# Two routed feed-forward layers merged into one block of programs each, and the first ternary unit split by operand part, in an eight-layer fp32 model kernel

## The chip, the cores and the metric

The kernel runs on one core of one Trainium2 chip. The metric is device time in microseconds (us) of one execution; three executions of the kernel before took 1485.39, 1490.49 and 1509.91 us, so the median is 1490.49 us. Lower is better.

## The reference

The input is a matrix of 1024 tokens by 256 features in fp32. Seven residual layers follow one another, each on the layer-normed stream: attention with 16 heads, a ternary feed-forward layer, a gated delta rule, the ternary layer again, attention, a routed feed-forward layer, latent attention with rotary parts, and the routed layer again. The change touches the two feed-forward kinds, each of which occurs twice.

```python
# ternary feed-forward: D = 256, DE = 1024; each weight is a sign in {-1, 0, 1} times one scale
up = jnp.einsum('bsd,ed->bse', x, wu)
gate = jnp.einsum('bsd,ed->bse', x, wg)
hidden = jax.nn.silu(up) * gate
return jnp.einsum('bse,de->bsd', hidden, wd)

# routed feed-forward: D = 256, hidden H = 704, 8 experts, 2 of them per token, low rank 16
for e in range(NUM_EXPERTS):
    c = jnp.sum(jnp.where(sf == e, wf, 0.0), axis=1)
    lo_up = LORA_ALPHA * (xt @ up_A[e].T @ up_B[e].T)
    lo_gate = LORA_ALPHA * (xt @ gate_A[e].T @ gate_B[e].T)
    h_e = jax.nn.silu(base_up + lo_up) * (base_gate + lo_gate)
    ch = c[:, None] * h_e
    mixed_h = mixed_h + ch
    lora_down = lora_down + LORA_ALPHA * (ch @ down_A[e].T @ down_B[e].T)
out = mixed_h @ w_down.T + lora_down
```

## The kernel before, in words

The residual stream X lies token by token in SBUF (8 tiles of 128 tokens), the normed stream XNT feature by feature (2 tiles of 128 features by 1024 tokens). Every engine runs a program of its own, written out by hand in the order in which its instructions issue; semaphores tie the programs together. A layer consists of one or more *blocks*: a block holds one program per engine, and no engine passes its end before all have reached it. `core.layer_done()` adds a barrier between layers. PSUM has 8 banks of 128 by 512 fp32.

**Ternary layer (`ternary_ffn`, lines 281 to 399, one block, twice).** The weights are signs in bf16. To keep fp32 accuracy the normed input is split into three bf16 parts, high, middle and low (`XP`): ScalarE copies XNT to bf16 (line 337, `x_high`), VectorE subtracts it (line 363, `x_rest`), ScalarE rounds the rest (line 340, `x_mid`), VectorE subtracts again (line 367, `x_low`). This is done for each of two halves of 512 tokens and each of two feature tiles k. Then 16 units (8 tiles of hidden features by two halves) follow: TensorE multiplies up and gate, 6 matmuls of 128x512 each (three parts by two k, line 318), into PSUM bank pair u % 2; ScalarE applies silu (line 346); VectorE forms the hidden value (line 376, `hid`); both split it in three parts for the down product. The first unit of a half waits for `x_low`, and unit u waits for `hid` of unit u - 2. The down product follows, with the norm of the next layer behind it (class `Norm`).

**Routed layer (`routed_ffn`, lines 1988 to 2268, two blocks, twice; the second one, `r1`, ends the kernel).** In the first block TensorE makes router logits, then for 11 pairs (5 hidden tiles for each half of the tokens, and one of 64 features that holds both halves, in partitions 0 to 63 and 64 to 127) the base product of up and gate and, in 22 steps, the low-rank corrections of the first and second expert slot (line 2103). ScalarE applies silu (line 2135), VectorE multiplies weight, gate and silu (lines 2193 and 2198, semaphore `hid`), GpSimd adds the two slots to `mixed_hidden` (line 2115). In the second block TensorE forms the low-rank down sums: 4 matmuls over the 64-row tiles (line 2224), then 20 over the full tiles (line 2229), into banks 0 to 3; VectorE masks and adds them (lines 2259, 2262). Then come 8 output tiles of 7 matmuls each (lines 2237, 2240, 2243) in banks 4 to 7, and the norm or the stores behind them. An fp32 matmul appears as two instructions in the trace. The SP queue loads the first weights of the latent layer at the start of the second block of the first routed layer (`r0`), and in `r1` it stores the result.

Of the kernel before, what the change touches and what calls it, by code (L numbers as in the profile page):

```python
# [10 lines left out]
ALU = mybir.AluOpType  # L11
# [269 lines left out]
def ternary_ffn(nc, core, tag, weights, loads):  # L281
# [7 lines left out]
    x_high, x_rest, x_mid, x_low = (sem("_x_" + n) for n in ("high", "rest", "middle", "low"))  # L289
    h_high, h_rest, h_mid, h_low = (sem("_h_" + n) for n in ("high", "rest", "middle", "low"))  # L290
    proj, act_done, hid, down, added = (sem(n) for n in ("_projected", "_silu", "_hidden", "_down", "_added"))
    with ExitStack() as tmp:
        XP = core.sb("xn_parts", [P, 3, KT, S], BF16, tmp)
        xr = core.sb("xn_rest", [P, KT, S], F32, tmp)
# [7 lines left out]
        with nc.Block() as block:  # L302
# [4 lines left out]
            @block.tensor  # L307
            def _(pe):
                for u, (e, half) in enumerate(units):
                    b = u % 2  # L310
                    if e == 0:
                        pe.wait_ge(x_low, KT * (half + 1))
                    if u >= 2:
                        pe.wait_ge(hid, u - 1)
                    for j, w in enumerate((ups, gates)):
                        for part in range(3):
                            for k in range(KT):
                                last = pe.matmul(psum[:, 2 * b + j, :], w[:, k, e * P:(e + 1) * P],  # L318
                                                 XP[:, part, k, cols(half)],
                                                 start=(part == 0 and k == 0), stop=(part == 2 and k == KT - 1))  # L320
                        last.then_inc(proj, 1)
# [12 lines left out]
            def _(act):  # L334
                for half in range(NH2):
                    for k in range(KT):
# [1651 lines left out]
def routed_ffn(nc, core, tag, w, router_loaded, loaded, all_loaded, next_loads, out_dram=None):  # L1988
# [9 lines left out]
    with ExitStack() as tmp:  # L1998
# [7 lines left out]
        with ExitStack() as tmp2:  # L2006
# [10 lines left out]
            Z = sb2("lora_in", [P, 2, TOPK, S])  # L2017
            sil, gc = sb2("silu", [P, 2, HALF]), sb2("gate_weighted", [P, 2, HALF])
            MD = sb2("mask_differences", [P, S])
            z_in, z_done, up_in, silu, gated, hid, mixed = (sem(n) for n in  # L2020
                ("z_in", "z_done", "up_in", "silu", "gated", "hidden", "mixed"))
            mask_diff = sem("mask_difference")
# [11 lines left out]
            steps = [(0, 0)] + [s for p in range(1, NP) for s in ((p, 0), (p - 1, 1))] + [(NP - 1, 1)]  # L2034
            at = {s: i for i, s in enumerate(steps)}
            with nc.Block() as block:
                @block.tensor
                def _(pe):
                    def lora_in(half):
# [45 lines left out]
                    for p, k in steps:  # L2085
# [15 lines left out]
                        for j, wl in enumerate(("upB", "gtB")):  # L2101
# [2 lines left out]
                                                 start=False, stop=True, skip_group_check=True)  # L2104
                            last.then_inc(up_in, 1)

                @block.gpsimd
                def _(pool):
                    pool.wait_ge(pmax, 1)
# [9 lines left out]
                def _(act):  # L2119
# [11 lines left out]
                    for i, (p, k) in enumerate(steps):  # L2131
                        act.wait_ge(up_in, 2 * i + 1)
                        if i >= 2:
                            act.wait_ge(hid, i - 1)
                        act.activation(sil[:, i % 2, :], psum[:, 2 * (p % BUF), :], ACT.Silu).then_inc(silu, 1)  # L2135

                @block.vector
                def _(dve):
# [61 lines left out]
                        if i == 0:  # L2200
                            lora_masked(1)


        with ExitStack() as tmp2:
            d1 = core.sb("lora_down_second", [P, S], F32, tmp2)
            d_in, d_part, d_done, out_in, added = sem("d_in"), sem("d_part"), sem("d_done"), sem("out_in"), sem("added")
            norm = Norm(core, tag, tmp2) if out_dram is None else None
            with nc.Block() as block:
                @block.sync
                def _(sp):  # L2210
                    if next_loads:
                        next_loads(sp)
                    if out_dram is not None:
                        for p in range(NT // 2):
                            sp.wait_ge(added, 2 * p + 2)
                            sp.dma_start(out_dram[2 * p * P:(2 * p + 2) * P, :].rearrange("(t p) d -> p t d", p=P),
                                         X[:, 2 * p:2 * p + 2, :]).then_inc(core.stored, 16)
                        sp.wait_ge(core.stored, 16 * (NT // 2))

                @block.tensor  # L2220
                def _(pe):
                    for k in range(TOPK):
                        for half in range(NH2):
                            pe.matmul(psum[:, 2 * half + k, :], w["dnA"][LAST[half], NFT - 1, :],  # L2224
                                      H[LAST[half], k, NFT - 1, 0:HALF], start=True, stop=False)
                    for half in range(NH2):
                        for k in range(TOPK):
                            for f in range(NFT - 1):
                                last = pe.matmul(psum[:, 2 * half + k, :], w["dnA"][:, f, :],  # L2229
                                                 H[:, k, f, half * HALF:(half + 1) * HALF],  # L2230
                                                 start=False, stop=(f == NFT - 2))
                            last.then_inc(d_in, 1)
                    for t in range(NT):
                        if t >= 4:
                            pe.wait_ge(added, t - 3)
                        for f in range(NFT - 1):
                            pe.matmul(psum[:, 4 + t % 4, 0:D], MX[:, f, t * P:(t + 1) * P], w["down"][:, f, :],  # L2237
                                      start=(f == 0), stop=False)
                        rows = LAST[t // 4]
                        pe.matmul(psum[:, 4 + t % 4, 0:D], MX[rows, NFT - 1, t % 4 * P:(t % 4 + 1) * P],  # L2240
                                  w["down"][rows, NFT - 1, :], start=False, stop=False)
                        pe.wait_ge(d_done, t // 4 + 1)
                        pe.matmul(psum[:, 4 + t % 4, 0:D], DL[:, t * P:(t + 1) * P], w["dnB"],  # L2243
                                  start=False, stop=True).then_inc(out_in, 1)
                        if norm:
                            norm.pe_behind(pe, t)

                if norm:
                    @block.scalar
                    def _(act):  # L2250
                        norm.act(act)

                @block.vector
                def _(dve):
                    for half in range(NH2):
                        cols = slice(half * HALF, (half + 1) * HALF)
                        for k, o in enumerate((DL, d1)):
                            dve.wait_ge(d_in, 2 * half + k + 1)
                            dve.tensor_tensor(o[:, cols], psum[:, 2 * half + k, :], MASK[:, k, cols],
                                              ALU.mult).then_inc(d_part, 1)  # L2260
                        dve.wait_ge(d_part, 2 * half + 2)
                        dve.tensor_tensor(DL[:, cols], DL[:, cols], d1[:, cols], ALU.add).then_inc(d_done, 1)
                    for t in range(NT):
                        dve.wait_ge(out_in, t + 1)
                        dve.tensor_tensor(X[:, t, :], psum[:, 4 + t % 4, 0:D], X[:, t, :], ALU.add).then_inc(added, 1)  # L2265
# [428 lines left out]
```

## Time and profile before

| quantity | value |
|---|---|
| median of three runs (lowest to highest) | 1490.49 us (1485.39 to 1509.91) |
| the profiled execution's own time | 1484.38 us |
| its span | 1482.7 us |
| TensorE busy | 1353.4 us, 91% of the span |
| VectorE / ScalarE / GpSimd busy | 60% / 47% / 19% |
| mean granted TensorE clock | 0.945 of full |
| lines 2224 to 2243 (chain that ended last) | about 3% of the span together |

The granted clock has two levels, 0.5 (1.2 GHz) and 1.0 (2.4 GHz) of full speed; a value between is a stretch that holds both. A busy TensorE at the lower level does half the work per microsecond. Matmuls overlap at their ends, so the distance from start to start, not the duration, says what one costs in a row of them. All windows are microseconds from the start of the span.

### The profile page before, as it was taken

How to read it: one execution, taken by the hardware profiler on the slowest of the kernel's cores; microseconds unless marked ns; L12 is line 12 of the kernel's file. 1: busy time of each engine (PE TensorE's matmuls, PEld its weight loads, DVE VectorE, ACT ScalarE, POOL GpSimd, SP SyncE). 2: the span in 40 equal slices, each digit the busy share in tenths (PEclk: the TensorE clock that was granted, in tenths of full speed). 3: DMA queues.
4: the chain of work that ended last, by engine and by line, in shares of the span. 5: the costliest groups of instructions: out<-in, count | busy, mean ns of one | idle time of the engine just before them, and what ended most of it. 6: DMA issues, size and time to landing. Idle time of an engine off the chain costs nothing. (4 is left out here: it accounts for less than half of the span.)

```text
span 1482.7 us, 32896 instructions
## 1 busy us (share of the span) xinstructions
PE 1353.4 (91%) x13705; PEld 749.8 (51%) x13705; DVE 891.5 (60%) x2142; ACT 696.5 (47%) x1042; POOL 277.6 (19%) x343
## 2 busy tenths in 40 slices
PE   7999997988679988989999989988699999989989
PEld 3355554464347773644555464445245555564436
DVE  3899994647484456649999555323455555526331
ACT  5577786636463226446777732102344444442110
POOL 4331431001510000043000001101433433200210
PEclk9999998999888989999999989999699999999999
DMA  3223301000300000032221030002100000000000
GB/s 88 66 35 68 68 3 32 2 2 0 114 2 4 16 1 15 1 61 34 37 42 24 3 104 0 0 9 48 20 12 17 15 13 15 7 1 1 1 0 29
DMA packets 33958, 37.48 MB, mean 25 GB/s; under 512 B 9153, under 2 KB 24626, under 8 KB 33810
## 3 DMA queue, kind: packets, MB, share of 16 engines
q1 hardware_dynamic: 33810, 35.39, 10.8%
q8 instruction: 108, 1.77, 0.5%
q14 instruction: 40, 0.33, 0.1%
HBM read 18.43 MB, written 1.07 MB: 13 GB/s over the span
## 5 line engine op out<-in xcount | busy, mean ns | idle before, releaser
L586 DVE TENSOR_REDUCE row_max_pieces<-psum 128x1 f32<-128x512 f32 (+3 forms) x672 | 407.0, 646 | 122.7 <-PE psum L481 120.4
L685 ACT ACTIVATE probs<-psum 128x1024 f32<-128x1024 f32 (+7 forms) x384 | 343.8, 900 | 219.7 <-PE psum L481 219.3
L535 PE MATMUL psum<-probs,v_ones 128*32 128x256 f32 (+1 forms) x2688 | 239.1, 376 | 8.6 <-POOL probs L470 4.2
L481 PE MATMUL psum<-q_all,k_head 97*32 97x512 f32 (+3 forms) x1536 | 193.8, 497 | 3.5 <-issue 3.5
L481 PE MATMUL psum<-k_stack,q_stack 96*32 96x512 bf16 x2048 | 162.7, 387 | 5.3 <-DVE row_max_pieces L586 3.1
L481 PE MATMUL psum<-q_stack,k_stack 97*32 97x512 bf16 x2048 | 160.8, 385 | 0.0
L535 PEld LDWEIGHTS psum<-probs,v_ones 128*32 128x32 f32 x2688 | 88.4, 109 | 85.3 <-POOL probs L470 20.9
L481 PE MATMUL psum<-k_head_bf,q_all_bf 80*32 80x512 bf16 (+3 forms) x768 | 95.3, 342 | 5.6 <-POOL q_all_bf L2511 3.7
L481 PEld LDWEIGHTS psum<-q_all,k_head 97*32 97x32 f32 x1536 | 79.2, 110 | 35.0 <-issue 9.3
L481 PEld LDWEIGHTS psum<-k_stack,q_stack 96*32 96x32 bf16 x2048 | 58.1, 97 | 72.1 <-DVE row_max_pieces L586 20.4
L481 PEld LDWEIGHTS psum<-q_stack,k_stack 97*32 97x32 bf16 x2048 | 59.2, 97 | 50.8 <-ACT probs L685 3.7
L2103 PE MATMUL psum<-lora_in,arena 128*128 128x512 f32 (+1 forms) x192 | 80.0, 595 | 3.4 <-DVE lora_in L2181 3.4
L2135 ACT ACTIVATE silu<-psum 128x512 f32<-128x512 f32 x44 | 26.3, 597 | 118.6 <-PE psum L2103 118.6
L2193 DVE TENSOR_TENSOR gate_weighted<-psum,weight_rows 128x512 f32<-128x512 f32 (+1 forms) x48 | 33.1, 690 | 78.6 <-PE psum L2103 78.5
L2053 PE MATMUL psum<-xn_features,arena 128*128 128x512 f32 (+1 forms) x192 | 79.4, 594 | 0.0
L481 PEld LDWEIGHTS psum<-k_head_bf,q_all_bf 80*32 80x32 bf16 x768 | 37.3, 97 | 52.1 <-issue 24.5
L318 PE MATMUL psum<-xn_parts,w_up_signs 128*128 128x512 bf16 x192 | 49.2, 394 | 10.5 <-DVE xn_parts L367 10.5
L470 POOL TENSOR_SCALAR_AFFINE_SELECT probs<-probs 128x128 f32<-128x128 f32 x128 | 36.9, 293 | 114.5 <-ACT probs L685 114.5
L2115 POOL TENSOR_TENSOR mixed_hidden<-slot_hidden 128x512 f32<-128x512 f32 x22 | 27.8, 1265 | 160.0 <-DVE slot_hidden L2198 160.0
L2103 PEld LDWEIGHTS psum<-lora_in,arena 128*128 128x128 f32 (+1 forms) x192 | 32.2, 181 | 46.8 <-issue 39.8
L2053 PEld LDWEIGHTS psum<-xn_features,arena 128*128 128x128 f32 (+1 forms) x192 | 32.4, 181 | 42.3 <-issue 40.7
L2508 POOL TENSOR_TENSOR q_all<-by_cos_over_by_sin,by_sin_moved 64x512 f32<-64x512 f32 x32 | 40.7, 1270 | 65.2 <-DVE row_max_pieces L586 39.5
(358 smaller groups left out, 2079.7 us busy)
## 6 DMA issues: line engine op xcount, KB each, us to landing
q_stack<-arena SPq DMA_DIRECT2D x32, 96.0 KB, 2.6
k_stack<-arena SPq DMA_DIRECT2D x32, 96.0 KB, 2.6
arena<-gd_g_sums SPq DMA_DIRECT2D x6, 512.0 KB, 6.1
q_stack<-arena SPq DMA_DIRECT2D x32, 64.0 KB, 2.3
k_stack<-arena SPq DMA_DIRECT2D x32, 64.0 KB, 2.3
x_tokens<-in_x SPq DMA_DIRECT2D x4, 256.0 KB, 3.4
k_stack<-arena SPq DMA_DIRECT2D x32, 32.0 KB, 2.3
q_stack<-arena SPq DMA_DIRECT2D x32, 32.0 KB, 2.1
```

The costliest lines, as they stand in the source:

```text
L318: last = pe.matmul(psum[:, 2 * b + j, :], w[:, k, e * P:(e + 1) * P], XP[:, part, k, cols(half)], start=(part == 0 and k == 0), stop=(part ...
L470: pool.affine_select(out=own, in_=own, compare_op=ALU.is_ge, fill=0.0, base=0, pattern=[[1, P]], channel_multiplier=-1).then_inc(masked, 1)
L481: last = pe.matmul(o[j:j + 32], by[:, j:j + 32], rows, **flags)
L535: last = pe.matmul(psum[32 * g:32 * g + VW, PVB, a - g * D:D], V[:, c, h, :], pr[:, n % PB, a:(g + 1) * D], start=(c == 0), stop=(c == (2 ...
L586: last = dve.reduce_max(mx[:, h % 2, qt, i:i + 1], o[:, 0:plain], AX.X)
L685: act.activation(pr[:, n % PB, q_from(c):], psum[:, 2 * (n % 2):2 * (n % 2) + 2, :].rearrange("p a n -> p (a n)")[:, q_from(c):], ACT.Exp, ...
L2053: pe.matmul(psum[rows, 2 * (p % BUF) + j, :], w[wb][:, kk, features], XNT[:, kk, cols], start=(kk == 0), stop=False, skip_group_check=True)
L2103: last = pe.matmul(psum[rows, 2 * (p % BUF) + j, :], w[wl][:, features], Z[:, j, k, cols], start=False, stop=True, skip_group_check=True)
L2115: pool.tensor_tensor(MX[:, f, cols], H[:, 0, f, cols], H[:, 1, f, cols], ALU.add).then_inc(mixed, 1)
L2135: act.activation(sil[:, i % 2, :], psum[:, 2 * (p % BUF), :], ACT.Silu).then_inc(silu, 1)
L2193: last = dve.tensor_tensor(gc[rows, i % 2, :], psum[rows, 2 * (p % BUF) + 1, :], CB[rows, k, cols], ALU.mult)
L2508: pool.tensor_tensor(Q[0:RD, h % QSLOTS, cols(half)], t[0:RD, i % 3, :], moved[:, i % 3, :], ALU.add).then_inc(added, 1)
```

## The change

In the routed layer the two blocks become one: each engine's second program is appended to its first, without the end of block between them. On TensorE the low-rank down sums follow the last up product in another order: the 10 matmuls of half 0, for whose hidden tiles they wait with `hid`; then the 4 of the 64-row tiles; then the 10 of half 1. Their banks are 6 and 7 for half 0, 4 and 5 for half 1 (`D_BANK`), and the output tiles use 6, 7, 4, 5 in turn (`OUT_BANK`), the first four of them after VectorE has read the sums (`d_part`). TensorE waits for GpSimd's `mixed` before the output tiles. The SP queue's loads and stores move into the merged block, so the latent layer's three loads are issued at the start of `r0`. The SBUF of both blocks is now reserved together.

In the ternary layer the copy of feature tile k = 1 to the high part moves from ScalarE to VectorE (semaphore `x_high_last`), and the first unit of a half runs part by part: up and gate of the high part after `x_high`, of the middle part after `x_mid`, of the low part after `x_low`.

```diff
+                    if e == 0:
+                        pe.wait_ge(x_high, half + 1)
+                        pe.wait_ge(x_high_last, half + 1)
+                        for j in range(2):
+                            product(j, 0)
+                        pe.wait_ge(x_mid, KT * (half + 1))
+                        for j in range(2):
+                            product(j, 1)
+                        pe.wait_ge(x_low, KT * (half + 1))
+                        for j in range(2):
+                            product(j, 2)
...
-                    for k in range(KT):
-                        act.activation(XP[:, 0, k, cols(half)], XNT[:, k, cols(half)], ACT.Copy).then_inc(x_high, 1)
+                    act.activation(XP[:, 0, 0, cols(half)], XNT[:, 0, cols(half)], ACT.Copy).then_inc(x_high, 1)
...
+                    dve.tensor_copy(XP[:, 0, 1, cols(half)], XNT[:, 1, cols(half)]).then_inc(x_high_last, 1)
                     for k in range(KT):
-                        dve.wait_ge(x_high, half * KT + k + 1)
+                        dve.wait_ge((x_high, x_high_last)[k], half + 1)
...
+            D_BANK, OUT_BANK = ((6, 7), (4, 5)), (6, 7, 4, 5)
...
+                    def lora_down(half):
+                        for k in range(TOPK):
+                            for f in range(NFT - 1):
+                                last = pe.matmul(psum[:, D_BANK[half][k], :], w["dnA"][:, f, :],
+                                                 H[:, k, f, half * HALF:(half + 1) * HALF],
+                                                 start=(half == 0 and f == 0), stop=(half == 1 and f == NFT - 2),
+                                                 skip_group_check=True)
+                            if half:
+                                last.then_inc(d_in, 1)
+
+                    pe.wait_ge(hid, at[NFT - 2, 1] + 1)
+                    lora_down(0)
+                    pe.wait_ge(hid, len(steps))
+                    for k in range(TOPK):
+                        for half in range(NH2):
+                            last = pe.matmul(psum[:, D_BANK[half][k], :], w["dnA"][LAST[half], NFT - 1, :],
+                                             H[LAST[half], k, NFT - 1, 0:HALF], start=(half == 1), stop=(half == 0),
+                                             skip_group_check=True)
+                            if half == 0:
+                                last.then_inc(d_in, 1)
+                    lora_down(1)
+                    pe.wait_ge(mixed, NP)
...
-        with ExitStack() as tmp2:
...
-            with nc.Block() as block:
```

TensorE at the start of a ternary layer (unit 0, then the next): `w_up_signs` and `w_gate_signs` are the two weights, `xn_parts` the three parts. Before:

```order
L307 UNCONDITIONAL_BRANCH
L318 MATMUL psum<-xn_parts,w_up_signs 128x512 x6
L318 MATMUL psum<-xn_parts,w_gate_signs 128x512 x6
L318 MATMUL psum<-xn_parts,w_up_signs 128x512 x6
L318 MATMUL psum<-xn_parts,w_gate_signs 128x512 x6
```

and now:

```order
L318 MATMUL psum<-xn_parts,w_up_signs 128x512 x2
L318 MATMUL psum<-xn_parts,w_gate_signs 128x512 x2
L318 MATMUL psum<-xn_parts,w_up_signs 128x512 x2
L318 MATMUL psum<-xn_parts,w_gate_signs 128x512 x2
L318 MATMUL psum<-xn_parts,w_up_signs 128x512 x2
L318 MATMUL psum<-xn_parts,w_gate_signs 128x512 x2
L318 MATMUL psum<-xn_parts,w_up_signs 128x512 x6
L318 MATMUL psum<-xn_parts,w_gate_signs 128x512 x6
```

The number of matmuls is the same; up and gate alternate by part in the first unit alone.

VectorE at the same place, now (before, the first and fourth rows are absent, and ScalarE makes both high copies):

```order
L377 CAST xn_parts<-xn_features 128x512
L380 TENSOR_TENSOR xn_rest<-xn_features,xn_parts 128x512 x2
L384 TENSOR_TENSOR xn_parts<-xn_rest,xn_parts 128x512 x2
L377 CAST xn_parts<-xn_features 128x512
L380 TENSOR_TENSOR xn_rest<-xn_features,xn_parts 128x512 x2
L384 TENSOR_TENSOR xn_parts<-xn_rest,xn_parts 128x512 x2
```

TensorE from the last up products of `r1` to the first output tile (`lora_in` enters the last corrections, `slot_hidden` the low-rank down sums). Before:

```order
L2103 MATMUL psum<-lora_in,arena 64x512 x4
L2036 UNCONDITIONAL_BRANCH
L2220 UNCONDITIONAL_BRANCH
L2224 MATMUL psum<-slot_hidden,arena 128x512 x4
L2229 MATMUL psum<-slot_hidden,arena 128x512 x20
L2237 MATMUL psum<-arena,mixed_hidden 128x256 x5
```

and now:

```order
L2135 MATMUL psum<-lora_in,arena 64x512 x4
L2143 MATMUL psum<-slot_hidden,arena 128x512 x10
L2155 MATMUL psum<-slot_hidden,arena 128x512 x4
L2143 MATMUL psum<-slot_hidden,arena 128x512 x10
L2169 MATMUL psum<-arena,mixed_hidden 128x256 x5
```

The branches out of one block and into the next are gone, and the 64-row matmuls (L2224, now L2155) stand between the two halves of the others.

## Rows read from the trace of the kernel before

**Rows 1.** Timeline (start, duration, engine, line, idle before) at the seam of `r0`.

```profile
961.29 5.67 PE L2103 MATMUL psum<-lora_in,arena 128*64 128x512 f32 x20
...
969.20 1.26 POOL L2115 TENSOR_TENSOR mixed_hidden<-slot_hidden 128x512 f32<-128x512 f32 x1 [1.07 <-DVE slot_hidden L2198]
...
970.82 3.50 PE L2224 MATMUL psum<-slot_hidden,arena 64*128 64x512 f32 x8 [3.86 <-PEq L2036]
...
991.52 2.32 PE L2237 MATMUL psum<-arena,mixed_hidden 128*128 128x256 f32 x10
```

**Rows 2.** Line 2103 on TensorE, durations min/median/max, first and last start: window 957:976, whole span.

```profile
L2103 PE MATMUL psum<-lora_in,arena x23: 592/592/697, 956.4 to 966.4; 128*64 128x512 f32 x16, 128*128 128x512 f32 x7
...
L2103 PE MATMUL psum<-lora_in,arena x192: 592/592/697, 894.1 to 1426.9; 128*128 128x512 f32 x160, 128*64 128x512 f32 x32
```

**Rows 3.** Timeline at the seam of `r1`.

```profile
1431.31 3.65 PE L2224 MATMUL psum<-slot_hidden,arena 64*128 64x512 f32 x8 [3.85 <-PEq L2036]
...
1452.17 2.32 PE L2237 MATMUL psum<-arena,mixed_hidden 128*128 128x256 f32 x10
```

**Rows 4.** Stretches: length, busy PE, PEld, DVE, ACT, POOL, granted clock, DMA share, GB/s.

```profile
970.80:973.00 2.20, 2.18 (x6) 1.24 (x8) 0.00 (x0) 1.26 (x1) 0.00 (x0) 0.50 0.43 119
973.00:974.00 1.00, 1.00 (x4) 0.03 (x1) 0.00 (x0) 0.00 (x0) 0.00 (x0) 0.55 0.06 11
...
1431.30:1434.00 2.70, 2.69 (x6) 1.25 (x8) 0.00 (x0) 0.00 (x0) 0.00 (x0) 0.50 0.00 0
1434.00:1435.00 1.00, 1.00 (x5) 0.10 (x1) 0.00 (x0) 0.00 (x0) 0.00 (x0) 0.65 0.00 0
```

**Rows 5.** Timeline in `r0`: cadence of sums and of one output tile.

```profile
978.22 0.19 PEld L2229 LDWEIGHTS psum<-slot_hidden,arena 128*128 128x128 f32 x1 [0.24 <-issue]
978.65 0.19 PEld L2229 LDWEIGHTS psum<-slot_hidden,arena 128*128 128x128 f32 x1 [0.24 <-issue]
...
994.93 2.32 PE L2237 MATMUL psum<-arena,mixed_hidden 128*128 128x256 f32 x10
...
998.35 2.32 PE L2237 MATMUL psum<-arena,mixed_hidden 128*128 128x256 f32 x10
```

**Rows 6.** Timeline at the start of the first ternary layer.

```profile
254.29 1.15 ACT L337 ACTIVATE xn_parts<-xn_features 128x512 bf16<-128x512 f32 x2 [1.13 <-PEq L70]
...
254.95 1.29 DVE L363 TENSOR_TENSOR xn_rest<-xn_features,xn_parts 128x512 f32<-128x512 f32 x2 [3.44 <-ACT xn_parts L337]
255.68 1.23 ACT L340 ACTIVATE xn_parts<-xn_rest 128x512 bf16<-128x512 f32 x2 [0.24 <-DVE xn_rest L363]
...
257.69 2.74 PE L318 MATMUL psum<-xn_parts,w_up_signs 128*128 128x512 bf16 x6 [5.16 <-DVE xn_parts L367]
...
258.27 1.23 ACT L340 ACTIVATE xn_parts<-xn_rest 128x512 bf16<-128x512 f32 x2 [0.32 <-DVE xn_rest L363]
...
260.81 0.69 ACT L346 ACTIVATE silu_up<-psum,ternary_scales 128x512 f32<-128x512 f32 x1
...
261.87 0.75 DVE L376 SCALAR_TENSOR_TENSOR hidden<-psum,ternary_scales,silu_up 128x512 f32<-128x512 f32 x1 [1.65 <-PE psum L318]
...
264.26 1.46 PE L318 MATMUL psum<-xn_parts,w_up_signs 128*128 128x512 bf16 x6
```

**Rows 7.** Timeline at the start of the second ternary layer.

```profile
567.86 2.74 PE L318 MATMUL psum<-xn_parts,w_up_signs 128*128 128x512 bf16 x6 [5.37 <-DVE xn_parts L367]
...
574.65 1.46 PE L318 MATMUL psum<-xn_parts,w_up_signs 128*128 128x512 bf16 x6
```

**Rows 8.** Stretches, columns as in rows 4, around the ternary starts and in the latent layer's setup.

```profile
253.70:255.00 1.30, 0.00 (x0) 0.00 (x0) 0.05 (x1) 0.71 (x2) 0.00 (x0) 0.50 0.06 13
...
1060.00:1080.00 20.00, 15.59 (x94) 5.30 (x97) 6.70 (x26) 5.21 (x7) 7.76 (x9) 0.51 0.04 7
```

**Rows 9.** Timeline: two VectorE copies in SBUF in the latent layer.

```profile
1033.55 0.42 DVE L2440 COPY w_q_rotary<-w_q_rotary 128x512 f32<-128x512 f32 x1
...
1038.91 0.69 DVE L2451 CAST k_features_bf<-k_features 128x1024 bf16<-128x1024 f32 x1 [2.36 <-ACT k_features L2414]
```

More of the change, by code:

```diff
@@ L310, in _, with product @@
                     b = u % 2
-                    if e == 0:
-                        pe.wait_ge(x_low, KT * (half + 1))
                     if u >= 2:
                         pe.wait_ge(hid, u - 1)
-                    for j, w in enumerate((ups, gates)):
-                        for part in range(3):
-                            for k in range(KT):
[L318 to L321, printed above, removed]
+                    def product(j, part):
+                        w = (ups, gates)[j]
+                        for k in range(KT):
+                            last = pe.matmul(psum[:, 2 * b + j, :], w[:, k, e * P:(e + 1) * P],
+                                             XP[:, part, k, cols(half)],
+                                             start=(part == 0 and k == 0), stop=(part == 2 and k == KT - 1))
+                        if part == 2:
+                            last.then_inc(proj, 1)
+                    if e == 0:
[9 more added lines that the diff above has]
+                            product(j, 2)
+                    else:
+                        for j in range(2):
+                            for part in range(3):
+                                product(j, part)
                 for t in range(NT):
@@ L2019, in routed_ffn @@
             MD = sb2("mask_differences", [P, S])
+            d1 = sb2("lora_down_second", [P, S])
+            d_in, d_part, d_done, out_in, added = sem("d_in"), sem("d_part"), sem("d_done"), sem("out_in"), sem("added")
+            norm = Norm(core, tag, tmp2) if out_dram is None else None
+            D_BANK, OUT_BANK = ((6, 7), (4, 5)), (6, 7, 4, 5)
             z_in, z_done, up_in, silu, gated, hid, mixed = (sem(n) for n in
@@ L2036, in routed_ffn, with _ @@
             with nc.Block() as block:
+                @block.sync
+                def _(sp):
+                    if next_loads:
+                        next_loads(sp)
+                    if out_dram is not None:
+                        for p in range(NT // 2):
+                            sp.wait_ge(added, 2 * p + 2)
+                            sp.dma_start(out_dram[2 * p * P:(2 * p + 2) * P, :].rearrange("(t p) d -> p t d", p=P),
+                                         X[:, 2 * p:2 * p + 2, :]).then_inc(core.stored, 16)
+                        sp.wait_ge(core.stored, 16 * (NT // 2))
                 @block.tensor
@@ new lines, in _ @@
+                    lora_down(1)
+                    pe.wait_ge(mixed, NP)
+                    for t in range(NT):
+                        bank = OUT_BANK[t % 4]
+                        if t < 4:
+                            pe.wait_ge(d_part, t + 1)
+                        else:
+                            pe.wait_ge(added, t - 3)
+                        for f in range(NFT - 1):
+                            pe.matmul(psum[:, bank, 0:D], MX[:, f, t * P:(t + 1) * P], w["down"][:, f, :],
+                                      start=(f == 0), stop=False)
+                        rows = LAST[t // 4]
+                        pe.matmul(psum[:, bank, 0:D], MX[rows, NFT - 1, t % 4 * P:(t % 4 + 1) * P],
+                                  w["down"][rows, NFT - 1, :], start=False, stop=False)
+                        pe.wait_ge(d_done, t // 4 + 1)
+                        pe.matmul(psum[:, bank, 0:D], DL[:, t * P:(t + 1) * P], w["dnB"],
+                                  start=False, stop=True).then_inc(out_in, 1)
+                        if norm:
+                            norm.pe_behind(pe, t)
@@ L2201, in _ @@
                             lora_masked(1)
-        with ExitStack() as tmp2:
-            d1 = core.sb("lora_down_second", [P, S], F32, tmp2)
-            d_in, d_part, d_done, out_in, added = sem("d_in"), sem("d_part"), sem("d_done"), sem("out_in"), sem("added")
-            norm = Norm(core, tag, tmp2) if out_dram is None else None
-            with nc.Block() as block:
[L2209 to L2254, printed above, removed]
@@ L2264, in _ @@
                         dve.wait_ge(out_in, t + 1)
[L2265 removed]
+                        dve.tensor_tensor(X[:, t, :], psum[:, OUT_BANK[t % 4], 0:D], X[:, t, :], ALU.add).then_inc(added, 1)
                         if norm:
```

6 lines of the change are left out of this document (4 added, 2 removed).

## The prediction

> **What bounds the kernel now.** I read the totals of the page first: TensorE is busy for 91% of the span and the other engines for 60% at most, so a gain has to come out of TensorE's idle time or out of its stretches at the lower clock. Then the timeline at the four places that the change touches, and the granted clock of the same stretches.
>
> At the seam inside a routed layer [rows 1, 3] the reader sees a hole on TensorE: after the last corrections (line 2103) it sits idle for 3.86 us in `r0` and 3.85 us in `r1`, released by the end of the block. The last thing that the end of the block waits for is GpSimd's sum of the two slots, 969.20 + 1.26 = 970.46, and TensorE starts at 970.82. Nothing in the first 10 low-rank sums needs that sum or even the last up product: they read hidden tiles of half 0. The hole has a second price [rows 4]: the granted clock is 0.50 when TensorE resumes, in `r0` until about 973.9 (0.55 over 973 to 974 means slow for 0.9 of it) and in `r1` until about 1434.7 (0.65 over 1434 to 1435, slow for 0.7).
>
> At the start of a ternary layer [rows 6, 7] TensorE waits 5.16 and 5.37 us for the low part of its input, while the high part has been there since about 254.95. It then starts at the lower clock: [rows 8] show 0.50 from 253.7 on, and six matmuls take 2.74 us, where at the higher clock six take 1.46 us.
>
> **The merged routed block.** Costs from start to start: full-height fp32 matmul instructions follow each other by 978.65 - 978.22 = 0.43 us [rows 5]. The output tile shows what a change between full-height and half-height tiles costs: tiles follow by 998.35 - 994.93 = 3.42 us, their 14 instructions of 256 columns are half of 0.43 each, 3.0 us, and two changes remain, 0.2 us each.
>
> In `r0` the last correction starts at 966.4 [rows 2]; 0.43 for itself and 0.2 for the change of tile shape give 967.0 as the first low-rank sum's start, against 970.82: 3.8 us. Its wait for `hid` is for a step some ten steps old. The lower clock goes as well, since TensorE does not stop: 973.9 - 970.82 = 3.1 us at half rate, of which half, 1.55 us, comes back. Against that stands one change of tile shape more, because the 64-row matmuls now have full-height ones on both sides: -0.2 us. Net 5.15 us. In `r1` the last correction starts at 1426.9 [rows 2], so the first sum would start at 1427.5 instead of 1431.31 [rows 3], 3.8 us; the clock gives (1434.7 - 1431.31) / 2 = 1.7 us; the change of shape -0.2. Net 5.3 us. Both layers 10.45 us. That the whole stretch up to the first output tile then shrinks from 20.7 us [rows 1] to about 19.3 us (40 instructions by 0.43, the eight half-height ones in pairs as four by 0.43, two changes) is the same account.
>
> Could a new wait take this back? The wait for the whole `hid` stands behind 20 instructions, 8.6 us: it is reached at 975.6, and GpSimd's sum, which needs the last `hid`, was over at 970.46 [rows 1]. The wait for `mixed` comes another 10 us later. VectorE gets half 0's sums while TensorE multiplies half 1's, so `d_part` and `d_done` are early: half 0's are due about 976.5 to 978.5 and the first output tile starts near 986.3. Bank 4 and 5 are read by VectorE within about 2 us of 986.3, and the third output tile, the first to use one, comes 6.8 us after the first. ScalarE has nothing between its last silu and the norm, so a table load there is covered. The SP queue's three loads move from 970 to about 868 in `r0`; their reader starts at 1024, and their tiles are free in both cases. I cost them at nothing; with the routed weights still in flight they would delay only the router's start. Ending a block later or earlier costs the other engines nothing, since TensorE is last in the merged one too.
>
> **The ternary starts.** Now: ScalarE copies k = 0 (254.29 to 254.9) and VectorE k = 1 at the same time. VectorE's copy is not in this trace; the nearest rows [rows 9] are an fp32 copy of 128x512 in 0.42 us and a cast of twice the size in 0.69 us, so it lies between 0.35 and 0.69; I take 0.42, the row of the same size. Either way TensorE can start at about 254.97, 2.7 us sooner. Its four high matmuls at half rate (0.427) end at 256.7. The middle part is ready at 255.68 + 1.23 = 256.91 [rows 6], a stop of 0.3 us; the low part is ready at 257.63 as before, when TensorE is still at the middle. So far the unit gains 2.4 us or more.
>
> But what ends the gain is unit 2, which needs the hidden value of unit 0, and that needs silu, which ScalarE can only begin after its share of half 1's split. That chain becomes longer: VectorE's copy for half 1 stands ahead of its subtraction, and ScalarE's rounding follows the subtraction directly [rows 6] (the second row of line 340, idle until VectorE). Silu 0, with its table load ahead, moves from 260.81 to 260.81 + 0.36 (a copy of 0.42, less the overlap of queued VectorE instructions) = 261.17; it takes 0.69, and VectorE's product, 0.75, ends at 262.65. TensorE starts unit 2 at about 262.7 instead of 264.26: 1.55 us, the most that the first layer can give. In the second, unit 2 started 574.65 - 567.86 = 6.79 us after unit 0 [rows 7], against 6.57 in the first, so the most is 1.75 us.
>
> Whether TensorE itself is ready at 262.7 is the clock's affair. In the four cases at hand (both ternary starts and [rows 4]) the clock came back 2.9 to 3.4 us after TensorE resumed. If it moves with the earlier start, to about 258.1, units 0 and 1 are over by 261.9 and the caps of 1.55 and 1.75 hold: 3.3 us. If it stays where it was, at 260.6 (8 slow matmuls and the fast ones after them), units 0 and 1 end at 257.0 + 3.6, with 12.4 matmuls done and 11.6 to go at 0.215, so at 263.1: 1.2 us in each layer, 2.4 in all. I take the middle, 2.9 us. The Trainium skill ("TensorE: Matmul & The Clock Gate", Part 1: The HAM clock gate) says that the point of return depends on where the first matmul lands and not on the number of matmuls, which speaks for the second value: by it the sum is 0.5 us smaller. The trace does not decide, since the return came at 2.9 us in one case and 3.4 in another.
>
> From unit 2 on nothing changes: TensorE needs 2.59 us for a unit (264.26 for the first start of unit 2, and six matmuls in 1.29), and the others need less.
>
> **The sum.** 1484.38 - 10.45 - 2.9 = 1471.0 us for an execution like the profiled one. That one is 1.0 us under the fastest of the three timed runs and 6.1 under their median; I add 1.0 for the offset and forecast 1472 us. With the ternary caps it is 1471.6, with the clock staying 1472.5, and with VectorE's copy at 0.69 some 0.5 us more.
>
> **Rivals.** (a) *The half-height matmuls do not run in pairs at the higher clock, or the tile changes cost more.* At the lower clock eight of them take 3.50 us [rows 1], 0.43 each, which can only be pairs of 0.86; at the higher one I count pairs of 0.43. Against: pairs in the corrections' last tile already run so (20 instructions in 5.67 us). If they stay at 0.43 each, 1.7 us per layer is lost: 1475 us. Chance 0.10. (b) *The merged programs do not do what they say*: TensorE is held at the seam by a stop that the trace of before hides under the block's end, for one the last `hid` if the sums of half 0 were not ready. Twice 3.8 us are lost then, 1472 + 7.6 = 1480 us, and with the clock down again 3 us more. The hidden values of half 0 were made tens of microseconds before, so 0.05. (c) *Clock for the better elsewhere.* In the latent layer's setup TensorE runs at 0.51 of the clock for 20 us while busy for 15.6 of them [rows 8]; everything there comes 8 us earlier now. If such a stretch returns to the higher clock early, up to 15.6 / 2, about 8 us, is gained: 1464 us. Nothing says which way it goes, so 0.10. (d) *Slower.* The same mechanism turned round: the gated delta rule and the latent setup both have gaps on TensorE, and if the shift leaves it at the lower clock for longer there, each microsecond of busy TensorE costs half of one. It decides from 2 x 13.3 = 27 us of added low clock on; with 40 us the time is 1485.4 + 20 - 13.3 = 1492 us. The longest such stretch of before is about 20 us, so 0.04. The forecast itself has the remaining 0.71.
>
> **Numbers.** 1472 us. The range 1463 to 1483 holds the forecast with its bounds (1469 to 1475), (a), (b) and (c), and the few microseconds by which a median of timed runs stands above the profiled execution; outside are (d) and runs above 1483. A change of 2%, about what a measurement of this kernel can tell from none, would be 30 us; the forecast is 1.2% under the median of before. For over 2% faster, (c) would have to come at both places: 0.04. Over 2% slower needs more than (d): 0.02. Within 2%: 0.94.
>
> **What would show it.** Right: TensorE without idle time between the last corrections and the first low-rank sum, granted clock 1.00 there, and about 19.3 us from that sum to the first output tile, in both routed layers; TensorE's first ternary matmul at 2.7 us less after the layer's start, a stop of about 0.3 us before the middle part, and unit 2 behind VectorE's product with TensorE idle for less than 1 us before it. Wrong: idle time at the seam with `hid` as its releaser; the 64-row group at 0.43 us each; silu 0 later than 0.7 us against before; or a difference in the attention or delta stages, with another clock, larger than 3 us.

## The result

The changed kernel took 1475.03 us (median of four runs, 1469.18 to 1498.48; three of them lie between 1469.18 and 1478.69); its ratio to the kernel before is 0.990 (95% interval 0.9873 to 0.9926). Run again over five rounds it gave 0.9909 (0.9877 to 0.9941). So it is 0.9 to 1.0% faster, and both intervals lie wholly under 1. The profiled execution took 1471.36 us (span 1469.6), against 1484.38 (1482.7). Some executions of these kernels are about 20 us longer, in the traces of `e4`, `e6`, `e8` and `e9` by a delta stage of 256 to 259 us at a mean granted clock of 0.79 against 234 to 238 us at 0.87 to 0.89; the ratios leave them out, and why they were seven of twelve in `e8` (median of all 1487.91 us) is open.

Each layer ends with the norm of the next one. Cut at the end of each norm into stages, the traces give this, length in us and mean granted clock (the last two columns are the runs `e1` and `e2`, described below):

| stage | before | change | change again | routed part only | ternary part only |
|---|---|---|---|---|---|
| attention A | 238.87 (0.98) | 237.63 (0.99) | 237.63 (0.99) | 239.39 (0.98) | 237.89 (0.99) |
| **ternary, first** | 73.64 (0.94) | 72.13 (0.95) | 72.04 (0.95) | 73.65 (0.94) | 72.09 (0.95) |
| delta rule | 236.32 (0.87) | 234.13 (0.89) | 237.48 (0.87) | 236.13 (0.88) | 237.87 (0.87) |
| **ternary, second** | 73.86 (0.95) | 72.06 (0.97) | 72.05 (0.97) | 73.91 (0.94) | 72.52 (0.95) |
| attention C | 229.91 (0.97) | 228.54 (0.98) | 228.49 (0.98) | 230.13 (0.97) | 231.94 (0.96) |
| **routed r0** | 156.88 (0.95) | 151.61 (0.97) | 151.61 (0.97) | 151.65 (0.96) | 158.02 (0.94) |
| latent | 303.72 (0.94) | 309.53 (0.92) | 304.32 (0.93) | 304.27 (0.93) | 309.11 (0.92) |
| **routed r1** | 155.20 (0.96) | 149.68 (0.97) | 150.64 (0.95) | 150.61 (0.95) | 154.97 (0.95) |

The four touched stages lose 1.5, 1.8, 5.3 and 5.5 us, 14.1 in all; the others, whose programs did not change, differ by -1.2, -2.2, -1.4 and +5.8, at another mean granted clock each.

The seam of `r0` in the timeline of the change (start, duration, engine, line, idle before), answering to [rows 1, 2]:

```profile
953.15 5.67 PE L2135 MATMUL psum<-lora_in,arena 128*64 128x512 f32 x20
...
958.75 8.85 PE L2143 MATMUL psum<-slot_hidden,arena 128*128 128x512 f32 x20
...
961.06 1.26 POOL L2188 TENSOR_TENSOR mixed_hidden<-slot_hidden 128x512 f32<-128x512 f32 x1 [1.07 <-DVE slot_hidden L2273]
967.53 1.99 PE L2155 MATMUL psum<-slot_hidden,arena 64*128 64x512 f32 x8
...
969.45 8.85 PE L2143 MATMUL psum<-slot_hidden,arena 128*128 128x512 f32 x20
...
978.14 2.32 PE L2169 MATMUL psum<-arena,mixed_hidden 128*128 128x256 f32 x10
```

No TensorE row has idle time in its bracket. GpSimd's last sum, which the end of the block used to wait for, now starts 2.3 us into 8.8 us of low-rank sums and ends 3.6 us into them. The eight half-height matmuls take 1.99 us, not 3.50. From the last corrections' first matmul to the first output tile it is 978.14 - 953.15 = 24.99 us; before, 991.52 - 961.29 = 30.23. In `r1` it is the same, with the row of before first and two of the change behind it:

```profile
1421.79 5.67 PE L2103 MATMUL psum<-lora_in,arena 128*64 128x512 f32 x20
...
1414.16 5.67 PE L2135 MATMUL psum<-lora_in,arena 128*64 128x512 f32 x20
...
1439.14 2.32 PE L2169 MATMUL psum<-arena,mixed_hidden 128*128 128x256 f32 x10
```

That is 1439.14 - 1414.16 = 24.98 us, and 1452.17 - 1421.79 = 30.38 before, with the output tile of [rows 3]. The trace of the change again (`e5`) has 24.99 us at both seams. The granted clock (stretch, length, busy PE, PEld, DVE, ACT, POOL, clock, DMA share, GB/s) at both seams, against 0.50 in [rows 4]:

```profile
958.80:967.50 8.70, 8.70 (x22) 3.68 (x20) 2.07 (x3) 1.11 (x1) 2.46 (x2) 1.00 0.00 0
...
1419.80:1439.10 19.30, 19.30 (x50) 8.29 (x49) 4.84 (x7) 0.00 (x0) 2.47 (x2) 1.00 0.00 1
```

The start of the first ternary layer, answering to [rows 6]:

```profile
253.05 0.63 ACT L353 ACTIVATE xn_parts<-xn_features 128x512 bf16<-128x512 f32 x1 [1.13 <-PEq L70]
253.07 0.43 DVE L377 CAST xn_parts<-xn_features 128x512 bf16<-128x512 f32 x1 [2.80 <-PEq L70]
...
253.73 1.03 PE L318 MATMUL psum<-xn_parts,w_up_signs 128*128 128x512 bf16 x2 [2.44 <-ACT xn_parts L353]
...
259.11 1.58 PE L318 MATMUL psum<-xn_parts,w_up_signs 128*128 128x512 bf16 x6
...
259.90 1.51 ACT L362 ACTIVATE silu_up<-psum,ternary_scales 128x512 f32<-128x512 f32 x2
...
261.82 1.46 PE L318 MATMUL psum<-xn_parts,w_up_signs 128*128 128x512 bf16 x6
```

and of the second, answering to [rows 7]:

```profile
559.53 0.63 ACT L353 ACTIVATE xn_parts<-xn_features 128x512 bf16<-128x512 f32 x1 [1.35 <-PEq L70]
...
563.52 0.59 PE L318 MATMUL psum<-xn_parts,w_up_signs 128*128 128x512 bf16 x2
...
566.39 1.26 ACT L362 ACTIVATE silu_up<-psum,ternary_scales 128x512 f32<-128x512 f32 x2
...
568.00 1.47 PE L318 MATMUL psum<-xn_parts,w_up_signs 128*128 128x512 bf16 x6 [0.87 <-DVE hidden L393]
```

The last row of each is unit 2. In the trace of before the first bf16 copy of the second layer is this row (that of the first is in [rows 6]):

```profile
564.46 1.15 ACT L337 ACTIVATE xn_parts<-xn_features 128x512 bf16<-128x512 f32 x2 [1.34 <-PEq L70]
```

Counted from the first bf16 copy unit 2 starts at 8.77 us (9.97 before) and at 8.47 (10.19 before): gains of 1.20 and 1.72. The silu of unit 0 (silu 0) starts at 6.85 and 6.86 us. The granted clock of three stretches, columns as above, says when the clock came back:

```profile
253.70:257.40 3.70, 3.56 (x8) 1.02 (x9) 3.60 (x7) 1.79 (x4) 0.00 (x0) 0.50 0.82 235
...
259.10:260.40 1.30, 1.30 (x7) 0.63 (x6) 0.21 (x1) 1.29 (x2) 0.00 (x0) 0.90 0.00 0
...
562.20:563.50 1.30, 1.30 (x4) 0.53 (x5) 1.30 (x4) 0.46 (x1) 0.00 (x0) 0.64 0.16 55
```

A mean of 0.90 over 1.3 us is 0.26 us at the lower level, so the clock came back at 259.4 in the first layer; 0.64 is 0.94 us, so at 563.1 in the second. In the first layer the whole of unit 0 ran at the lower clock (5.4 us from 253.73 to 259.11) and TensorE has no idle time before unit 2: the clock was the limit. In the second the clock was back in the middle of unit 0, and TensorE idles 0.87 us for the hidden value: the silu chain was the limit.

### The profile page after: what moved, and what is told of

The parts are those of the page before. It is cut to its first block and busy times, and to the rows that moved or that the text cites. A ratio compares the mean times of both kernels' runs of the same rounds, so it can differ in the third digit from the quotient of the medians.

```text
span 1469.6 us, 32878 instructions
## 1 busy us (share of the span) xinstructions
PE 1352.2 (92%) x13705; PEld 746.5 (51%) x13705; DVE 893.1 (61%) x2146; ACT 694.1 (47%) x1038; POOL 277.0 (19%) x343
```

## The experiments

**Routed part alone** (`e1`): the changed kernel with the ternary function of before.

> The changed kernel with the ternary layer of before: only the merged routed block is left. My account of the seam (3.8 us of idle time, 1.6 us of clock, less 0.2 us, per layer) expects 10.5 us under the kernel before, ratio 0.993, and each routed layer 5.2 to 5.5 us shorter in its trace. The rival that the gain of the whole comes from a luckier clock in layers nobody touched expects the routed layers to shorten all the same, but the total to differ from 10.5 us by whatever delta and latent do (they moved by -2.2 and +5.8 us in the changed kernel).

Measured: ratio 0.9932 (0.9912 to 0.9951), about 10 us; `r0` 5.2 and `r1` 4.6 us shorter, every other stage within 0.6 us of before (table). The stage of `r1` gained less than the 5.2 to 5.5 us expected, here as in the change again, at a mean granted clock of 0.95 where the first trace of the change has 0.97; its seam was the same. The account of the seam holds without any help from the layers nobody touched.

**Ternary part alone** (`e2`): the kernel before with the changed ternary function.

> The kernel before with the ternary layer of the change. My account expects 2.9 us less in all (2.4 to 3.3), ratio 0.998, which is at the limit of what five rounds tell from none; in the trace unit 2 of each layer starts 1.2 to 1.75 us earlier after the first bf16 copy. If the gain in the first ternary layer is set by the clock and in the second by silu, as the trace of the changed kernel reads, TensorE idles before unit 2 only where its clock came back within some 3.5 us of its start.

Measured: 0.9994 (0.9974 to 1.0014), not told from no change. Its ternary stages are 1.55 and 1.34 us shorter, as expected; but latent came out 5.4 and attention C 2.0 us longer in its trace. The lower clock lasted until unit 1 in both layers, and no idle time stands before unit 2, which starts 8.75 and 8.95 us after the first copy: the limit was the clock twice. The run tests the ternary part as a whole; what the copy on VectorE and the order part by part give each by itself was not run.

**What the idle time at the seam costs in clock** (`e3`): the kernel before, and behind the last corrections

```diff
+                    for _ in range(4):
+                        pe.matmul(psum[:, 2 * BUF, :], ident[:], XNT[:, 0, 0:HALF], start=True, stop=True)
```

> The kernel before with four fp32 matmuls of 128x512 added on TensorE behind the last corrections, ahead of the end of the first routed block: identity by the normed stream, into bank 6, never read. They fill the 3.8 us of idle time with work that serves nothing. If the lower clock after the seam is the price of the idle time, the granted clock stays 1.00, the eight half-height matmuls take about 1.9 us instead of 3.5 and the kernel gains 1.5 us per layer, 3 us in all, less 0.1 to 0.3 us per layer if the added work ends after GpSimd's sum. If the clock falls for another reason (the end of a block as such), there is no gain and perhaps 0.5 us of loss.

The timeline on TensorE, and the clock of the half-height matmuls:

```profile
967.85 3.70 PE L2107 MATMUL psum<-xn_features,identity 128*128 128x512 f32 x8
971.85 1.99 PE L2226 MATMUL psum<-slot_hidden,arena 64*128 64x512 f32 x8 [0.30 <-PEq L2036]
```

```profile
971.80:973.80 2.00, 1.95 (x9) 0.81 (x9) 0.00 (x0) 1.28 (x1) 0.00 (x0) 1.00 0.42 108
```

The end of the block is still there and the clock stays up, so the end of a block does not lower it by itself; with TensorE idle for 3.86 us there it fell, with 0.30 us it did not. The half-height group takes 1.99 us instead of 3.50. From the corrections' first row to the first output tile both layers gain, 1.4 us in `r0` and 1.6 in `r1`; the stages are 1.46 and 0.78 us shorter. The times do not bear this out: the ratio is 0.9997 (0.9985 to 1.0009), and the 3 us expected, 0.998, lie just outside. In the trace latent took 307.2 us, 3.5 more than before, so what the clock is worth at the seam rests on the seams of the traces alone.

**Merge without the new order** (`e4`): the changed kernel with the half-height sums first, behind `hid` of the last step.

> The changed kernel, but the low-rank sums in the order of before: the four over the 64-row tiles first, behind the wait for the last hidden value, then the twenty others. It splits the gain of the merge from that of the new order. TensorE waits from about 966.8 to 969.2 in the time of the trace of before, 2.4 us per layer; one change of tile shape less gives 0.2 us back. If the clock stays up over 2.4 us: 2.2 us per layer more than the changed kernel, 4.4 us in all. If the clock falls there too: 3.8 us per layer, 7.6 us in all, and almost nothing is left of the merge but its 1.5 us of idle time per layer.

```profile
985.63 1.99 PE L2142 MATMUL psum<-slot_hidden,arena 64*128 64x512 f32 x8 [2.22 <-DVE slot_hidden L2264]
```

TensorE waits 2.22 us for the last hidden value and the clock stays up (1.99 us again). From the corrections' first row to the first output tile it takes 27.07 us in both layers, 2.1 us more than with the change; the stages are 153.71 and 151.82 us. Of the 5.3 us in `r0` the merge alone gives 3.2 and the order 2.1. Ratio 0.9941 (0.9916 to 0.9966), as expected above that of the change, though its interval and those of the change overlap.

**The change again** (`e5`), unaltered:

> The changed kernel itself, unaltered, for a narrower interval and a second trace. My account expects 13.4 us less than before, ratio 0.991, and the four touched stages 1.5, 1.8 or 1.3, 5.3 and 5.5 us shorter as in its first trace. The latent stage took 303.7 us in the trace of before and 309.5 in that of the change. If that is a cost of the change (its loads issued 100 us earlier, or the place where the layer now starts), it is again 309 to 310 us; if it is the clock's chance, it lies anywhere between 303 and 311.

Its latent stage took 304.32 us, against 309.53 in the first trace; the three rows of the latent stage, before, change and change again, differ in granted clock and busy TensorE, not in the number of its instructions:

```profile
1023.78:1327.50 303.72, 279.54 (x3168) 146.10 (x3168) 158.59 (x580) 127.50 (x213) 103.39 (x200) 0.94 0.09 18
```

```profile
1010.39:1319.92 309.53, 286.13 (x3168) 148.52 (x3168) 158.64 (x580) 127.39 (x214) 103.02 (x200) 0.92 0.09 18
```

```profile
1013.74:1318.06 304.32, 282.26 (x3168) 147.02 (x3168) 158.65 (x580) 127.50 (x214) 103.21 (x200) 0.93 0.10 18
```

The same program has it either way, so the difference is no price of the change. One stretch at the lower clock makes it up (first trace of the change, then the change again):

```profile
1042.00:1074.00 32.00, 27.59 (x157) 10.91 (x161) 11.88 (x45) 7.65 (x10) 11.01 (x15) 0.50 0.03 5
...
1045.00:1068.00 23.00, 18.59 (x85) 7.12 (x89) 8.80 (x34) 4.90 (x7) 10.13 (x12) 0.50 0.03 7
```

With its ends it lasts 34.1 us (1041.0 to 1075.1) in the one and 23.9 us (1044.4 to 1068.3) in the other. These are 10.2 us more at the lower clock, with TensorE busy for most of them, and the stage is 5.2 us longer. What ended the stretch later in the one is open.

**The latent layer's loads where they were** (`e6`): `sp.wait_ge(mixed, NP)` ahead of `next_loads(sp)`.

> The changed kernel, but the SP queue waits for GpSimd's last sum of the slots before it issues the latent layer's three loads, which puts them where they stood before. If their early issue costs anything (in the router's start or in the latent stage), this one is faster than the changed kernel by it, 5.8 us if the whole of the latent stage's difference hangs on it. I expect no difference, within 1.5 us of the changed kernel.

Measured 0.9905 (0.9882 to 0.9928), the change's own ratio; `r0` 151.29 us, latent 305.59. Their earlier issue costs nothing that can be seen.

**Three more copies in the silu chain** (`e10`, one execution), ahead of the second half's copy:

```diff
+                    if half:
+                        for e in (NE - 3, NE - 2, NE - 1):
+                            dve.tensor_copy(HP[:, 2, e, cols(half)], XNT[:, 1, cols(half)])
```

> The changed kernel with three more VectorE copies of 128x512 to bf16 (into a tile that is written over later) ahead of the one that begins the second half's split, so the suspected step of the silu chain is four times its size. If unit 2 waits for silu 0 and that for VectorE's copies, silu 0 starts 3 x 0.35 = 1.05 us later, 7.9 us after the first bf16 copy instead of 6.85, and unit 2 starts 9.4 to 9.5 us after it in both ternary layers, instead of 8.77 and 8.47, whatever the clock does. If the clock alone sets the start of unit 2, it stays between 8.4 and 8.8.

The first bf16 copy of the first layer starts at 254.40, of the second at 564.26; unit 2 in each:

```profile
263.89 1.47 PE L318 MATMUL psum<-xn_parts,w_up_signs 128*128 128x512 bf16 x6 [0.58 <-DVE hidden L396]
...
573.73 1.47 PE L318 MATMUL psum<-xn_parts,w_up_signs 128*128 128x512 bf16 x6 [0.20 <-DVE hidden L396]
```

9.49 and 9.47 us after the copy, with silu 0 at 7.87 and 7.86: both as expected, although the clock came back 6.2 us after the copy in one layer and 7.0 in the other. Unit 2 starts at the later of two things, TensorE's own readiness and the chain through VectorE's copy and silu 0.

**The second half's split later** (`e7`): its eight operations go, one by one, behind units 1 to 5 (on VectorE `later = {1: lambda: high(1), 2: lambda: rest(1, 0), ...}`).

> The changed kernel, but in the ternary layer the split of the second half of the tokens is spread over the first units on ScalarE and VectorE instead of standing ahead of them. Silu of unit 0 then follows its table load at about 3.9 us after the first bf16 copy instead of 6.85. If that chain is what TensorE idles for before unit 2 (0.87 us in the second ternary layer's trace, nothing in the first, where the clock was late), this gains 0.9 us there and nothing in the first: 1 us in all, not to be told from the changed kernel by the times, but the idle time before unit 2 must be gone. If VectorE or ScalarE has no room for the eight operations among the units, TensorE waits for hidden values in units 3 to 8 instead and the layer is longer by up to 5 us.

The second ternary layer, unit 1's gate and unit 2:

```profile
565.97 1.46 PE L318 MATMUL psum<-xn_parts,w_gate_signs 128*128 128x512 bf16 x6
567.27 1.46 PE L318 MATMUL psum<-xn_parts,w_up_signs 128*128 128x512 bf16 x6
```

The idle time is gone, unit 2 starts 7.45 us after the first copy instead of 8.47, and that stage takes 71.44 us instead of 72.06; the first stage is unmoved (72.11). As expected the times don't show it: 0.9913 (0.9899 to 0.9927).

**TensorE kept busy in the norms' gaps** (`e8`), on top of `e7`, behind each of the last two groups of transposes:

```diff
+                for _ in range((5, 5)[p - self.PAIRS + 2]):
+                    pe.matmul(self.core.psum[:, spare, 0:P], self.core.ident[:], self.core.ones_sq[:], start=True, stop=True)
```

> The kernel with the later split, and besides 5 small fp32 matmuls (identity by a matrix of ones, 128x128, never read) behind each of the last two groups of transposes in every norm that follows a product. They occupy TensorE in gaps of 1.5 us where it has nothing to do. If the lower clock at the start of the ternary and routed layers comes from these gaps, it stays up: the ternary layer's first two units take 5.2 us instead of up to 8.1 (2 to 2.5 us per layer), and the router's 32 narrow matmuls take 3.5 us instead of 7, so up to 10 us over the kernel, less 0.3 us per norm (seven norms) by which the last group delays the end of the block. If the barrier between the layers is what lets the clock fall, nothing is gained and 2 us are lost.

Measured 0.9887 (0.985 to 0.9924), an interval that overlaps that of `e7`. The router's 32 narrow matmuls take 4.50 us in `r0` instead of 6.81 in the change, but the clock falls while they run, and the first products behind them (6.25 us, 5.53 in the change) are slower. Still `r0` takes 150.49 us and `r1` 146.98, against 151.61 and 149.68 to 150.64 in the two traces of the change. In the first ternary layer the clock fell in unit 0, 2.1 us after a start at the higher level, and nothing was gained there (72.51 us). In the second it stayed up throughout, and the stage takes 71.05 us.

**And in the gaps of the ternary start** (`e9`), three small matmuls ahead of unit 0 and three before its middle part:

> The kernel with the later split and the filled norm gaps, and besides three small fp32 matmuls (never read) on TensorE ahead of the first unit of the ternary layer and three more between its high and its middle part, which fill the 0.9 and 0.95 us that the trace of the kernel with filled norm gaps shows there. If the clock then stays at 1.00 through units 0 and 1, each ternary layer's first two units end 1 to 1.7 us earlier and the whole is 2 to 3 us under that kernel. If it falls all the same, the six small matmuls cost up to 1.4 us per layer and the ternary stages are longer.

```profile
256.53 0.59 PE L324 MATMUL psum<-xn_parts,w_up_signs 128*128 128x512 bf16 x2
...
262.77 1.46 PE L324 MATMUL psum<-xn_parts,w_up_signs 128*128 128x512 bf16 x6
```

```profile
255.80:262.80 7.00, 6.78 (x37) 3.86 (x38) 3.75 (x6) 4.92 (x8) 0.00 (x0) 1.00 0.52 172
```

These rows are of the first ternary layer. The clock stays at 2.4 GHz through units 0 and 1, and the ternary stages take 70.83 and 71.05 us (72.51 and 71.05 in `e8`, 72.13 and 72.06 in the change). So the six added matmuls gained 1.7 us in the first layer and nothing in the second, where the clock had stayed up without them; the expectation had a gain in each. `r1` takes 150.24 us, so its gain in `e8` was not repeated. Ratio 0.9846 (0.9809 to 0.9882), median 1465.14 us: the lowest here. Its interval meets that of the repeated change only in the last 0.05%, but overlaps that of `e8` widely, so the times do not tell `e9` from `e8`.

## Why the prediction was right and wrong

*The seam.* Forecast: first sum 5.7 us after the corrections' first row (966.4 + 0.63 - 961.29), 19.3 us from there to the first output tile, 5.15 and 5.3 us gained. Measured: the first sum at 5.60 us, then 978.14 - 958.75 = 19.39; gained 30.23 - 24.99 = 5.24 in `r0` and 30.38 - 24.98 = 5.40 in `r1`. The whole stage of `r1` gained 5.5 us in the first trace and 4.6 in the other two, at a lower mean clock there. Two parts show by themselves: the clock's 1.5 us in the traces of `e3`, though not in its times, and in `e4` the wait for the last hidden value (2.2 us of the 3.8 of the whole stop; the rest is GpSimd's sum and the end of the block). Half-height matmuls do run in pairs at the higher clock, so rival (a) fell, and with no stop at the seam so did (b).

*The ternary starts.* Forecast 2.9 us between 2.4 and 3.3; measured at unit 2, 1.20 + 1.72 = 2.92; the two stages are 3.3 us shorter, and the 0.4 us between the two are not accounted for. That 2.9 came out is partly luck: I took the middle of two cases, and the first layer hit the clock's bound (1.2) and the second the silu chain's (1.75). In `e2` both layers hit the clock's, 1.22 and 1.24. The chain's own figures held: VectorE's cast takes 0.43 us (forecast 0.42), silu 0 came at 6.85 us (forecast 6.88), and `e10` moved it as computed. I let the clock return at 258.1 or 260.6, that is 3.1 or 5.6 us after TensorE resumed, the same in both layers. It returned after 5.6 us in the first (259.4 - 253.7) and 2.9 in the second (563.1 - 560.2), so each value was right in one layer. The trace of before had shown no case longer than 3.4, and the four cases of it could not tell the two apart.

*What else moved.* The loads, which I costed at nothing, cost nothing that `e6` shows. The untouched stages moved by +1.0 us in sum, but alone by -2.2 to +5.8. Rivals (c) and (d) named the mechanism, a luckier or unluckier clock in delta and latent, and (d) took the longest stretch at the lower clock to be about 20 us; it is 23.9 us in the trace of before (1055.8 to 1079.7) and 34.1 in the first of the change. The two traces of the change differ by 3.4 us in delta and 5.2 in latent, so this is scatter between executions of one program, and no run shows it as an effect of the change.

*The step that failed* is the last one, the reading of size: "A change of 2%, about what a measurement of this kernel can tell from none". The sum was 13.35 us against an execution of 1484.38, 0.90%, and 0.90 to 1.00% was measured. But I set 1472 against the median of before, which stood 6 us above the profiled execution, called that 1.2%, and by the 2% treated it as a change that would not be told from none, with 0.94 for a result within 2%. The 2% had no row behind it. The measured intervals reach 0.1 to 0.4% either way (the change itself 0.27 and 0.32%), so a change of 1% can be told, and was: 0.990 (0.9873 to 0.9926), faster. With a sum resting on idle time that the trace shows four times, "faster by about 0.9%" was the forecast to make. The predicted time itself, 1472, was 3 us under the median of the four runs, inside its range, and next to the profiled execution's 1471.36. The mechanism and the terms of the sum held.

## What to carry to other kernels

The seam between these two blocks cost its idle time of 3.9 us and then 1.5 us more at the lower clock; independent work (here half of the next stage's sums) put directly behind the last product removed both, and merging alone, without that order, left 40% of the gain behind. When work is released part by part, look for the second chain that becomes the limit, here silu behind the next half's preparation, and move that preparation too. Add up a forecast against the profiled execution stage by stage, and judge it stage by stage: a stage whose program did not change differed by 5.2 us between two executions of the change, as much as the whole gain at one seam. And before calling a forecast too small to be measured, look up how wide the intervals of the measurement are.

## What the runs showed of the hardware

A stop of 2.22 us behind busy TensorE (`e4`) left the granted clock at 1.00, one of 3.86 us (before) brought it to 0.50. The length of the last stop alone does not decide: in the change the first ternary unit came 2.44 us after the last transpose, and the clock had already fallen about 1.2 us after that transpose (0.73 over 251.5 to 253.7). There TensorE had been busy for only 2.9 us of the 6.5 us from 246.0 to 252.5. With the gaps of the norm filled (`e8`) the clock was still 1.00 at the start of both ternary layers.

Thirty-two narrow matmuls (128x8), with TensorE busy throughout by the profile, did not hold the clock in `e8`: it fell from 1.00 to 0.50 about 2.7 us into them in `r0`. After a return of TensorE from a stop, the clock came back after 2.8 to 3.4 us in the kernel before, after 2.9 and 5.6 us in the change, and after 5.6 and 6.3 us in `e10`. In `e9`, six small square matmuls ahead of and inside unit 0 went with a clock of 1.00 in the first ternary layer, where it fell in `e8`; that is one trace of each, and in the second layer it stayed up in both.
